# A dispatch loop with one stage more, GpSimd's bias split moved, and gathered rows weighed on another engine

## The reference

```python
x = x + tanh(g_xattn[0]) * L0_xattn(layernorm(x), ctx, ...)     # stage 0: 32 heads, windows, ALiBi
# stage 1: mixture of 8 experts, top 2
logits = xf @ router_w.T
topk_vals, topk_idx = top_k(logits, 2)
topk_weights = softmax(topk_vals)
gate, value = silu(xf @ w1[e]), xf @ w2[e]
expert_out = (gate * value) @ w3[e]
x = x + tanh(g_ffn[0]) * sum(expert_out[topk_idx] * topk_weights)
x = x + tanh(g_xattn[1]) * L1_xattn(layernorm(x), ctx, ctx)     # stage 2: 8 heads over 256 channels
x = x + tanh(g_ffn[1]) * L1_ffn(layernorm(x), gate_w, expert_w, expert_b)   # stage 3: needs expert_b
...                                                             # stages 4 to 7
```

## Time and profile before

| | |
|---|---|
| median of 3 runs | 1421.21 us (1420.57 to 1421.45) |
| profiled execution | 1435.09 us, its span 1433.3 us |
| busy: PE, DVE, ACT, POOL | 80%, 65%, 36%, 30% of the span |
| granted TensorE clock, mean | 0.937 |
| stage 0 | from the start to about 333 us |
| stage 1 | to about 445 us, its loop from about 354 us |
| stage 2 | to about 645 us |

### The profile page before, as it was taken

The page is one execution under the profiler, slowest core; times in us unless marked ns, Lnnn a source line. Parts: engine busy times, 40 slices in busy tenths (PEclk is TensorE's granted clock), DMA queues, the critical chain, the costliest instruction groups (busy, mean ns, idle before and its releaser), DMA issues.

```text
span 1433.3 us, 34532 instructions
## 1 busy us (share of the span) xinstructions
PE 1152.3 (80%) x12364; PEld 908.6 (63%) x12364; DVE 925.5 (65%) x2510; ACT 512.3 (36%) x946; POOL 430.9 (30%) x940
## 2 busy tenths in 40 slices
PE   0699889883774677887898799998566699999998
PEld 0477666662663344445666666666454599999998
DVE  1367666656665598976766577778566666565665
ACT  0355555553331355562000223232115433333332
POOL 2254555546844876511100111113032100000000
PEclk9899999996997699998999999999689899999999
DMA  7222222402654445321000100000105200000000
GB/s 296 100 68 69 83 83 83 138 24 71 206 163 126 114 130 137 108 82 59 1 0 0 30 22 22 15 22 7 38 0 171 86 1 16 2 15 1 0 15 16
DMA packets 90935, 93.94 MB, mean 66 GB/s; under 512 B 10100, under 2 KB 83220, under 8 KB 90428
## 3 DMA queue, kind: packets, MB, share of 16 engines
q1 hardware_dynamic: 84924, 78.23, 17.5%
q0 software_dynamic: 5024, 13.67, 3.2%
q10 hardware_dynamic: 864, 0.43, 0.1%
HBM read 56.76 MB, written 35.53 MB: 64 GB/s over the span
## 4 chain that ended last, share of the span: by engine, by line
PE 55%; DVE 21%; issue 11%; POOL 4%; ACT 4%; DMA 2%; another core or an unknown queue 2%; DVEq 1%; SPq 1%; ACTq 0%; POOLq 0%
PE psum L2269 5%; PE psum L1345 4%; PE psum L1347 4%; PE psum L1346 4%; PE psum L986 3%; DVE mx L1934 2%; PE psum L1363 2%; DVE mx L756 2%; PE psum L1365 2%; PE psum L1364 2%; PE psum L949 1%; PE psum L969 1%; DVE mx L2161 1%; DMA rows<-in_rows 1%
## 5 line engine op out<-in xcount | busy, mean ns | idle before, releaser
L659 POOL TENSOR_SCALAR veps<-mv 128x1 f32<-128x1 f32 x112 | 26.3, 235 | 723.9 <-DVE mv L1213 375.3
L1345 PE MATMUL psum<-xnTh,w7h 128*128 128x256 f32 x512 | 147.4, 288 | 0.0
L1346 PE MATMUL psum<-xnTl,w7h 128*128 128x256 f32 x512 | 146.0, 285 | 0.0
L1347 PE MATMUL psum<-xnTh,w7l 128*128 128x256 f32 x512 | 145.9, 285 | 0.0
L756 DVE TENSOR_REDUCE mx<-psum 128x6 f32<-128x960 f32 (+3 forms) x80 | 80.7, 1009 | 75.4 <-PE psum L954 51.4
L1422 ACT ACTIVATE sil<-psum 128x256 f32<-128x256 f32 x128 | 49.3, 385 | 195.4 <-PE psum L1347 195.4
L1445 DVE TENSOR_TENSOR hTf<-sil,psum 128x256 f32<-128x256 f32 x128 | 53.9, 421 | 97.8 <-ACT sil L1422 92.1
L1347 PEld LDWEIGHTS psum<-xnTh,w7l 128*128 128x128 f32 x512 | 99.3, 194 | 0.0
L1345 PEld LDWEIGHTS psum<-xnTh,w7h 128*128 128x128 f32 x512 | 99.1, 193 | 0.0
L1346 PEld LDWEIGHTS psum<-xnTl,w7h 128*128 128x128 f32 x512 | 99.0, 193 | 0.0
L1934 DVE TENSOR_REDUCE mx<-psum 128x4 f32<-128x1024 f32 x64 | 77.0, 1205 | 26.6 <-PE psum L1998 21.4
(11 more groups left out here) (349 smaller groups left out, 3212.1 us busy)
## 6 DMA issues: line engine op xcount, KB each, us to landing
xs<-qpad SPq DMA_DIRECT2D x17, 1024.0 KB, 4.8
ctxT<-in_ctxT SPq DMA_DIRECT2D x48, 128.0 KB
ext<-qscr SPq DMA_DIRECT2D x96, 64.0 KB
w_raw<-in_w SPq DMA_DIRECT2D x16, 384.0 KB, 3.4
arena<-in_w SPq DMA_DIRECT2D x1, 5120.0 KB, 21.7
PT<-xs SPq DMA_DIRECT2D x39, 128.0 KB, 2.4
ys<-yt SPq DMA_DIRECT2D x39, 128.0 KB, 2.0
q_parts<-kscr SPq DMA_DIRECT2D x66, 64.0 KB
```

Source lines behind the costliest of these rows:

```text
L1345: MM(o, wh, xnTh[:, s, c], start=(c == 0), stop=False)
L1346: MM(o, wh, xnTl[:, s, c], start=False, stop=False)
L1347: t = MM(o, wl, xnTh[:, s, c], start=False, stop=(c == NC - 1))
```

## The change

There are four edits.

At the start, `loaded_later` is divided: the table of the router (`tri`, `steer`, `wr`, `iota8`) has a semaphore of its own, `loaded_route`, and only DVE and PE of stage 0 wait for it. POOL's bias split is moved to the begin of stage 1, its reload into the context loop, and the weights `w13` are loaded in four pieces beside turns 2, 5, 8 and 11 of stage 0, each clear of `xs` coming one turn later.

The dispatch loop gets one stage more: `down` follows two tiles behind `up` and not one. The engines' orders in a turn are changed with it, the drain to `yt` goes from DVE to ACT, PE loads registers in groups of four, and the rounding of weights goes in single instructions, one a tile for 28 tiles.

In stage 2, tiles 0 and 1 are combined, normalised and split by DVE alone. From tile 2 on, ACT multiplies the two gathered rows with their weights (`weigh`), POOL adds them (`sum_rows`), and DVE adds the sum to x in one instruction. POOL's gathers go from the begin of its turn to behind `sum_rows`, and the two clears of the value buffers go to stage 1.

```diff
@@ s0_sp
+            def weights(k):
+                m = 10240 // W13_PIECES
+                sp.dma_start(arena[:, m * k:m * (k + 1)], a["w13"][:, m * k:m * (k + 1)]).then_inc(w_loaded[1], 16)
             for n in range(NB - 2):
                 sp.wait_ge(F("qkv_psum").sem, F("qkv_psum").at(n, 1))
                 load(n + 2, n % 2)
-                clear(n)
-            for q in range(NB - 2, NB + 1):
+                if n >= 1:
+                    clear(n - 1)
+                if n % 3 == 2:
+                    weights(n // 3)
+            for q in range(NB - 3, NB + 1):
                 clear(q)
@@ combine, weigh, sum_rows, gather
-            dve.wait_ge(gathered[t % 4], 32 * (t // 4 + 1))
+            if t < 2:
+                dve.wait_ge(gathered[t], 32)
+                nc.vector.scalar_tensor_tensor(x[:, t], got[:, t, 0], wk_all[:, t, 0:1], x[:, t], ALU.mult, ALU.add).then_inc(summed.sem, 1)
+                dve.wait_ge(summed.sem, summed.at(t, 1))
+                o = nc.vector.scalar_tensor_tensor(x[:, t], got[:, t, 1], wk_all[:, t, 1:2], x[:, t], ALU.mult, ALU.add)
+            else:
+                dve.wait_ge(summed.sem, summed.at(t, 1))
+                o = nc.vector.tensor_tensor(x[:, t], x[:, t], got[:, t % 4, 0], ALU.add)
+            o.then_inc(combined.sem, 1)
+        def weigh(act, t):
+            act.wait_ge(gathered[t % 4], 32 * (t // 4 + 1))
             for k in range(2):
-                if k:
-                    dve.wait_ge(combined.sem, combined.at(t, 1))
-                nc.vector.scalar_tensor_tensor(x[:, t], got[:, t % 4, k], wk_all[:, t, k:k + 1], x[:, t], ALU.mult, ALU.add).then_inc(combined.sem, 1)
+                nc.scalar.activation(got[:, t % 4, k], got[:, t % 4, k], ACT.Identity, scale=wk_all[:, t, k:k + 1]).then_inc(weighed.sem, 1)
+        def sum_rows(pool, t):
+            pool.wait_ge(combined.sem, combined.at(1, 1))
+            pool.wait_ge(weighed.sem, weighed.at(t - 2, 2))
+            plain(pool)
+            nc.gpsimd.tensor_tensor(got[:, t % 4, 0], got[:, t % 4, 0], got[:, t % 4, 1], ALU.add).then_inc(summed.sem, 1)
...
@@ s0_dve and s0_pe
-                        dve.wait_ge(loaded_later, LOADS_1)
+                        dve.wait_ge(loaded_route, LOADS_R)
...
@@ s1_pe
-            for j in range(N_TILES + 1):
-                if 0 <= j - 1:
-                    transpose_h(j - 1)
+            for j in range(N_TILES + 2):
                 if j < N_TILES:
-                    up(j, units[j])
-                    unit_of(j + 1)
-                if 0 <= j - 1:
-                    down(j - 1, units.pop(j - 1))
+                    up(j, unit(j))
+                if 0 <= j - 1 < N_TILES:
+                    transpose_h(j - 1)
                 transposes(j + 2)
+                if 0 <= j - 2:
+                    down(j - 2, unit(j - 2))
+                    pe.free_register(units.pop(j - 2))
+                if j % UNIT_GROUP == UNIT_GROUP // 2 and UNIT_GROUP * (j // UNIT_GROUP + 1) < N_TILES:
+                    load_units(j // UNIT_GROUP + 1)
@@ s1_act
+                if 0 <= j - 2:
+                    act.wait_ge(d_psum.sem, d_psum.at(j - 2, 1))
+                    if j - 2 >= 3:
+                        act.wait_ge(y_out[(j - 2) % 3], 16 * ((j - 2) // 3))
+                    A.copy(yt[:, (j - 2) % 3], bank(6 + (j - 2) % 2)[:, 0:C]).then_inc(d_out.sem, 1)
@@ s1_dve
-                if n_stages > 4 and j in (14, 26):
-                    s4_weight_quant(dve, j // 26)
-            if n_stages > 4:
-                for q in (2, 3):
-                    s4_weight_quant(dve, q)
+                if n_stages > 4 and 10 <= j < 10 + 28:
+                    s4_weight_quant(dve, j - 10)
@@ s1_pool
+            pool.wait_ge(loaded_later, LOADS_1)
+            bias_split()
+            P.memset(tail[:, 0:816], 0.0).then_inc(v2_ready, 1)
...
             for b in range(NB):
+                if b == 4:
+                    bias_rows()
                 context(b, b % 2, b // 2)
...
-            for t in range(3):
+            for t in range(2):
                 gather(pool, t)
@@ s2_pool, body
                 if inside(n):
-                    if inside(n + 3):
-                        gather(pool, n + 3)
                     rs(n, 1 - s)
-                    normalise(n, 1 - s)
+                    if n >= 2:
+                        normalise(P, pool, n, 1 - s)
                 if inside(pp):
                     add(pp)
                 if inside(n):
-                    operands(n, 1 - s)
+                    if n >= 2:
+                        operands(P, pool, n, 1 - s)
+                    if 2 <= n + 1 < NB:
+                        sum_rows(pool, n + 1)
+                    for m in (2, 3) if n == 0 else (n + 3,):
+                        if m < NB:
+                            gather(pool, m)
                 if inside(b):
                     lay(b, s)
@@ s2_dve, body
                     ln_stats(2, dve, n, None, 1 - s)
+                    if n < 2:
+                        normalise(V, dve, n, 1 - s)
+                        operands(V, dve, n, 1 - s)
...
-                if i == -1 and n_stages > 4:
-                    s4_weights_dve(dve)
...
+            if n_stages > 4:
+                s4_weights_dve(dve)
             s2_turns(body)
@@ s2_act, body
                         nc.scalar.copy(qop[96:120, b % 3].rearrange("p (m e) n -> p m e n", e=2)[:, :, e], src).then_inc(F("mxT").sem, 1)
+                if 2 <= i + 4 < NB:
+                    weigh(act, i + 4)
@@ gpsimd
-                pool.dma_start(eb_n[:], a["eb"]).then_inc(eb_in, 16)
...
-                pool.wait_ge(loaded_later, LOADS_1)
-                s0_pool(pool)
+            s0_pool(pool)
+            fetch(0, 0)
+            fetch(1, 1)
```

More of the change, by code:

```diff
@@ L301, in bass_program @@
         w1_high, w1_low, w3_high, w3_low = sem("w1_high"), sem("w1_low"), sem("w3_high"), sem("w3_low")
-        w_loaded = [sem(f"w_loaded{k}") for k in range(8)]
+        w_loaded = {k: sem(f"w_loaded{k}") for k in (1, 3, 4, 5)}
         prep_w = Flag(sem("prep_w"), 0)
@@ L365, in bass_program @@
         gathered = [sem(f"gathered{k}") for k in range(4)]
-        combined = per_tile("combined", 2)
+        combined, summed, weighed = per_tile("combined"), per_tile("summed"), per_tile("weighed", 2)
         xt_in = [sem(f"xt_in{k}") for k in range(8)]
@@ L997, in body @@
                         pe.wait_ge(loaded_s0, 32)
-                        pe.wait_ge(loaded_later, LOADS_1)
+                        pe.wait_ge(loaded_route, LOADS_R)
                     wait("qkT", b, 3)
@@ L1161, in bass_program, with s4_weight_quant @@
         wprep_pe = sem("wprep_pe")
-        def s4_weight_quant(dve, n):
+        def s4_weight_quant(dve, i):
+            V = nc.vector
+            n, k = i // 7, i % 7
             w, o = n // 2, n % 2
-            k = 7 * n
-            if n == 0:
+            src, dst, tmp = wq_n[:, w, o], qw[:, w, o], qt_f[:]
+            sc = wsc[:, n].rearrange("p a b -> p (a b)")
+            if i == 0:
                 dve.wait_ge(w_loaded[4], 16)
             else:
-                dve.wait_ge(wprep.sem, k)
-            quant(dve, wq_n[:, w, o], qw[:, w, o], wsc[:, n].rearrange("p a b -> p (a b)"), qt_f[:], wprep, 0, k)
-            nc.vector.tensor_scalar(diag[:, n], ident[:], wsc[:, n].rearrange("p a b -> p (a b)")[:, 1:2], None, ALU.mult).then_inc(wprep.sem, 1)
+                dve.wait_ge(wprep.sem, i)
+            if k == 0:
+                t = V.tensor_reduce(sc[:, 0:1], src, axis=AX.X, op=ALU.max, apply_absolute_value=True)
+            elif k == 1:
+                t = V.tensor_scalar(sc[:, 1:2], sc[:, 0:1], 1.0 / 127.0, 1e-8, ALU.mult, ALU.max)
+            elif k == 2:
+                t = V.reciprocal(sc[:, 2:3], sc[:, 1:2])
+            elif k == 3:
+                t = V.tensor_scalar(tmp, src, sc[:, 2:3], 127.0, ALU.mult, ALU.min)
+            elif k == 4:
+                t = V.tensor_scalar(tmp, tmp, -127.0, MAGIC, ALU.max, ALU.add)
+            elif k == 5:
+                t = V.tensor_scalar(dst, tmp, MAGIC, None, ALU.subtract)
+            else:
+                t = V.tensor_scalar(diag[:, n], ident[:], sc[:, 1:2], None, ALU.mult)
+            t.then_inc(wprep.sem, 1)
         def s4_weights_dve(dve):
@@ L1518, in last @@
                     add(p, s, units - 1)
-                    if n_stages > 4:
-                        for q in range(4):
-                            s4_weight_quant(dve, q)
             pipeline(dve, first, body, last, n_items=NB // 2)
@@ L1593, in s1_pe, with load_units, unit @@
             pe.wait_ge(table_ready, TABLE_STEPS)
+            units = {}
+            def load_units(g):
+                regs = [pe.alloc_register(f"unit{g}_{k}") for k in range(UNIT_GROUP)]
+                pe.reg_load(regs, table[0:1, 1, UNIT_GROUP * g:UNIT_GROUP * (g + 1)])
+                for k, r in enumerate(regs):
+                    units[UNIT_GROUP * g + k] = r
```

(34 more changed lines are left out.)

68 lines of the change are left out of this document (31 added, 37 removed).

## The result

Timed side by side, the changed kernel has a median of 1427.31 us (1424.39 to 1433.04, 8 runs) and the kernel before 1421.37 (1420.57 to 1423.39): ratio 1.0042 [1.0025, 1.0060], 0.4% slower. Forecast were 1397, with 1372 to 1412 as the range. The forecast failed.

What follows compares the result with a forecast made beforehand. No engine bounds the whole run: stages wait for each other, each with its own limit. -24.1 - 19.1 - 4.1 + 23.0 = -24.3 us on 1435.1 gives 1410.8, scaled to the median 1397; range 1372 to 1412.

Steps and rivals of the forecast that it cites:

- Start, -24.1: Before stage 0: POOL's reciprocal root no longer waits for the late loads, 24.1 us less.
- "I cost them at nothing", the four pieces: Stage 0: the weights' four pieces, loaded beside turns of some 16 us, were taken to cost nothing.
- Loop, -19.1: Dispatch loop: PE's stand before `down` and the long rounding stands go; 38 steps take 66.4 us against 85.5.
- taken at 0.8: Dispatch loop: cost in us of PE's register load for each group of four, so 0.2 a tile.
- the rival's mechanism: Dispatch loop keeps 2.05 us a tile: loads queue behind stores one step later, PE waits again; total 1409, chance 0.12.
- Stage 2, start, -4.1: From first gather to first values matmul: fewer gathers go first and DVE does tiles 0 and 1, 4.1 us less.
- Turns, +23.0: Stage 2 turns: `lay` waits behind weighing, sum and gathers, so nine turns take 13.3 us; 23.0 us more in all.
- I take 0.6: Stage 2 turns: us added to each of nine turns for PE's low clock after its stand, 12.73 to 13.3.
- the bound of 1.7: Stage 2 turns: upper limit in us for the low-clock cost of a turn, from a stand in the loop.
- slower than before: Stage 2 rival: PE's clock stays at 1.2 GHz, nine turns of 16.7 us, +53.6, total 1427; chance 0.04.
- Nothing else moves: Stretches outside the start, loop and stage 2, including stage 7: forecast at 0 us difference.
- The level: Whole run: 1410.8 us from the profiled 1435.1 was scaled to the runs' median of 1421.2, giving 1397.

Runs made afterwards that it cites:

- e10_ahead: Changed kernel with `lay` first, weighing ahead of the copies, weights in one piece, SP's registers by four, loads seven tiles ahead: 1367.74 us, ratio 0.9538 to before.
- e14_single: e10_ahead with PE loading one register a tile in the dispatch loop instead of groups of four: 1370.23 us, ratio 0.9561 to before.
- e1_lay: Changed kernel with POOL's `lay` placed ahead of the sum and the two gathers in stage 2: 1406.73 us, ratio 0.9815 to before.
- the record profile: First profile of the changed kernel, no further edit: 1424.39 us, belonging to the lower of two time levels.
- e6_weigh: Changed kernel with `lay` first, weights in one piece and ACT's weighing ahead of the copies: 1378.48 us, ratio 0.9618 to before.
- e5_after: Changed kernel with no further edit, timed again beside the kernel before in a later session: 1437.20 us, ratio 1.0029.

## Why the prediction was wrong, step by step

*Start, -24.1.* Right: -24.0. Loads of tile 0 had the cover they were said to have.

*"I cost them at nothing", the four pieces.* Wrong by 13.4 us, 12.7 by the medians. The step asked only whether the weights would be there in time, not who else needs the DMA engines in those 10 us. The Trainium skill (Runtime: NRT & Kernel Launch, Instruction fetch mechanics) says that the sequencer fetches blocks of 16 KiB over a DMA queue of its own and that the cost is "mostly hidden". The trace agrees on the block and the queue; beside a bulk load it was not hidden, three times.

*Loop, -19.1.* Right in direction and cause (PE's stand for DVE went, PE alone needs 1.40, less than the 1.50 of the sum), too large in size: 1.82 and 1.89 a step for the 1.75 of the sum (66.4 over 38). It is not the register load that makes the rest, bounded from 0 to 3.4 us a group and taken at 0.8; by the steps it costs up to 0.35 where nothing else falls on it. The 0.84 behind that figure was misread: it is the whole gap between two of SP's issues in before, of which the load's own row is 0.27. The missing part is the rival's mechanism, a load behind a store that now comes a step later: 9.8 us of PE's waits. The rival said that it would keep 2.05 a tile; it cost 0.15 to 0.3. The rule of the Trainium skill cited in the forecast, 200 ns for each register, would make four registers 0.8; here the rows on SP's queue are 0.30 for four (e10_ahead) and 0.27 for one (before), and e14_single speaks for far less too.

*Stage 2, start, -4.1.* Right: -5.1.

*Turns, +23.0.* The mechanism was right to the hundredth (5.18 for 5.19) and its cure was e1_lay. The term that was mis-sized is the clock: "I take 0.6", measured 1.9 a turn. The stand came every turn, and the low clock with it in every turn, while the bound of 1.7 was made from one stand in the loop. This is 12 of the 17 us missed in the record profile. Another 5 lie in the turns of tiles 10 to 12 (12.6, 11.7, 10.4 for 10.3, 10.3, 9.3), part low clock, part the weighing that sits ahead of DVE's addition: e6_weigh shows this second ring, which the forecast missed because it followed `lay` alone. The rival "slower than before" named this clock mechanism with 16.7 us a turn. It came by 1.4 of the 3.4 us on the way there, and it needed the other two losses to end slower. That its number, 1427, is the measured one is luck.

*Nothing else moves.* Wrong in our favour: -7.7 in stage 7.

*The level.* Scaling a profile at 1435 to a median of 1421 by its ratio was unfounded. The two belong to two levels, and the gap is not spread evenly: in the changed kernel 10.7 of its 11.7 us lie in stage 0.

Together: +13.4, +6.3, -1.0, +15.2, -7.7 make the 26.2 us between -24.3 and +1.9. Two steps failed most: the pieces of the weights put at nothing, and the clock of the turns put at 0.6 where it took 1.9.

## What to carry to other kernels

Where a helper's work is queued, ask for every instruction behind it on its engine who waits for that; the same work one place later (e1_lay) or earlier (e6_weigh) was worth 45 us of 1437. A bulk load beside running compute has a price if instructions are fetched at the same time; put it where the engines stand anyway. A stand that repeated in every turn took the clock down in every turn here, so price such a stand at the low level for the work behind it, not as a remainder.

## What the runs showed of the hardware

- PE and DVE stand without a semaphore when instructions are late: PE 3.0 to 4.4 us beside three of four loads of 1280 KB (after, e5_after), up to 2.7 beside 640 KB; DVE 9.0 us in stage 7 of before, gone in every kernel with the change. The second is shown by the traces only, not by an experiment of its own. The Trainium skill (Runtime: NRT & Kernel Launch, Instruction fetch mechanics) warns of taken branches whose target lies outside the blocks at hand; stage 7 is a loop, and the packets in before fit that, but no run tests it.
- In stage 0 at the upper level, a reduction of DVE that reads PSUM and has stood for PE starts 0.2 to 0.5 us behind GpSimd's indirect scatters and not during them; at the lower level it starts during them. An instruction that follows another of DVE without a pause starts during them at the upper level too (in e5_after a reciprocal at 130.50, in the scatter from 129.95 to 130.91). The gathers of stage 2 do not hold it back at the upper level either: in before `mx` has stood 0.73 us and starts at 506.77, 0.5 us into the gather at 506.27. The Trainium skill (SBUF — State Buffer, Who interferes with whom) holds that on this chip `tensor_reduce` never contends with GpSimd. The record profile and the gathers agree with that, the waits of stage 0 do not, and their cause is not shown.
- A stand of 2.6 us of PE in every turn goes with a mean clock of 0.78; without it, in turns of 10.53 and 9.95, it is 1.00, and 0.96 in those of e1_lay.
- The fastest version that leaves nothing out, e10_ahead, has a ratio of 0.9538 to the kernel before, 66 us, with `lay` first, the weighing ahead of the copies, the weights whole at the start, SP's registers by four and loads seven ahead.
